# The router's products in four column groups with the gate stationary, and places counted by three products

## The reference, cut to what matters

```python
logits = xt @ gate_w.T                      # xt: 4096 x 256, gate_w: 8 x 256
scores = softmax(logits)
top_vals, idx = top_k(scores, 2)
weights = take_along_axis(scores, idx, axis=1)
xs = xt[:, None, :] * weights[:, :, None]
for e in range(8):
    mask = (idx == e)
    h  = silu(xs @ w1[e].T + b1[e])
    x2 = h @ w2[e].T + b2[e]
    x3 = xs @ w3[e].T + b3[e]
    y  = y + sum(x2 * x3 * mask)
z = silu(xt @ sw1.T) * (xt @ sw2.T) @ sw3.T  # the shared expert, for every token
out = x + gb * (y + z)
```

## Time and profile before

| | us |
|---|---|
| median of 3 runs | 2153.1 |
| span of the profiled execution, first to last instruction | 2151.5 |
| the stage of the change | about 1681 to 1900 |
| PE busy, whole span | 1868.9 (87%) |
| DVE busy, whole span | 1957.7 (91%) |
| ACT busy, whole span | 1522.9 (71%) |
| POOL busy, whole span | 1807.2 (84%) |

### The profile page before, as it was taken

How to read it: one execution, slowest core, us unless ns; L and a number is a source line. 1 busy time by engine, 2 the same in 40 slices (tenths; PEclk the granted TensorE clock), 3 DMA queues, 4 the chain that set the end, 5 groups by cost and what they waited for, 6 DMA issues and landing times.

```text
span 2151.5 us, 26056 instructions
## 1 busy us (share of the span) xinstructions
PE 1868.9 (87%) x6376; PEld 792.9 (37%) x6377; DVE 1957.7 (91%) x1814; ACT 1522.9 (71%) x3148; POOL 1807.2 (84%) x624
## 2 busy tenths in 40 slices
PE   7879898988889898989898888889775799999998
PEld 3323232323233332323232323333221466655554
DVE  7999999999999999999999999999999777557776
ACT  5786879798888879786878888887956333434443
POOL 5689999999999999999999999999999333415444
PEclk9998898989899898989898998989876899999999
DMA  6736445353625354454536263545334652234444
GB/s 261 248 108 159 104 125 124 101 127 102 153 73 149 96 142 109 124 123 110 129 101 140 80 156 88 135 109 129 98 102 134 237 186 79 107 82 79 78 78 70
DMA packets 140347, 265.32 MB, mean 123 GB/s; under 512 B 21264, under 2 KB 44048, under 8 KB 139072
## 3 DMA queue, kind: packets, MB, share of 16 engines
q1 hardware_dynamic: 125488, 242.05, 41.2%
q0 software_dynamic: 13440, 17.93, 4.9%
q10 hardware_dynamic: 1296, 3.93, 0.5%
HBM read 194.51 MB, written 70.39 MB: 123 GB/s over the span
## 4 chain that ended last, share of the span: by engine, by line
POOL 30%; PE 25%; issue 17%; ACT 14%; DVE 11%; DVEq 2%; DMA 0%; POOLq 0%; ACTq 0%; SPq 0%
POOL hst L940 21%; POOL dbu L928 7%; ACT psum L1257 6%; PE psum L2188 5%; PE psum L2031 4%; DVE hst L1611 4%; PE psum L2200 3%; PE psum L2251 2%; POOL dt L920 2%; PE psum L1951 2%; PE psum L1979 2%; DVE dbu L1590 1%; PE psum L1963 1%; ACT dbu L1289 1%; PE psum L2271 1%
## 5 line engine op out<-in xcount | busy, mean ns | idle before, releaser
L940 POOL TENSOR_TENSOR hst<-hst,c_rep 128x2048 f32<-128x2048 f32 x254 | 1143.7, 4521 | 4.2 <-ACT state L1243 4.2
L1611 DVE TENSOR_TENSOR_SCAN hst<-psum,state,dbu 128x1024 f32<-128x1024 f32 x384 | 878.8, 2330 | 6.2 <-ACT psum L1257 5.6
L1257 ACT ACTIVATE psum<-dt_rep,neg_a 128x512 f32<-128x512 f32 (+1 forms) x1024 | 659.8, 676 | 136.4 <-DVE hst L1611 131.4
L1590 DVE TENSOR_TENSOR dbu<-psum,b_rep 128x2048 f32<-128x2048 f32 x176 | 398.7, 2265 | 9.8 <-PE psum L2016 9.7
L928 POOL TENSOR_TENSOR dbu<-dtu_rep,b_rep 128x2048 f32<-128x2048 f32 x80 | 362.6, 4532 | 9.1 <-DMA dtu_rep<-dtu_scratch 4.9
L2031 PE MATMUL psum<-hst,same 128*32 128x512 f32 x2048 | 282.7, 701 | 84.1 <-POOL hst L940 77.9
L1611 DVE TENSOR_TENSOR_SCAN hst<-psum,dbu 128x1024 f32<-128x1024 f32 x128 | 286.4, 2272 | 11.9 <-ACT psum L1257 11.4
L2016 PE MATMUL psum<-dt,same 32*128 32x512 f32 x352 | 216.1, 696 | 91.4 <-DVE dbu L1590 85.8
L1963 PE MATMUL psum<-xp,taps 128*128 128x512 f32 x512 | 235.8, 604 | 7.3 <-ACT sp_tmp L1226 7.3
L1050 POOL DMA_INDIRECT out_x<-h,target_u x72 | 112.3, 1560 | 152.7 <-DMA out_x<-h,target_u 75.5
L2031 PEld LDWEIGHTS psum<-hst,same 128*32 128x32 f32 x2048 | 67.7, 126 | 306.6 <-issue 169.5
(11 more groups left out here) (186 smaller groups left out, 2512.8 us busy)
## 6 DMA issues: line engine op xcount, KB each, us to landing
dt_rep<-dt_scratch SPq DMA_DIRECT2D x256, 256.0 KB, 4.7
dtu_rep<-dtu_scratch SPq DMA_DIRECT2D x320, 64.0 KB, 1.9
taps<-taps_scratch SPq DMA_DIRECT2D x64, 256.0 KB, 4.4
b_rep<-bc_scratch SPq DMA_DIRECT2D x64, 256.0 KB, 5.0
c_rep<-bc_scratch SPq DMA_DIRECT2D x64, 256.0 KB, 7.7
dt_scratch<-dt SPq DMA_DIRECT2D x63, 256.0 KB, 5.4
h<-slot_scratch SPq DMA_DIRECT2D x72, 129.5 KB
sp_tmp<-t_scratch SPq DMA_DIRECT2D x16, 512.0 KB, 6.8
```

The lines of the kernel that those rows point to most:

```text
L940: nc.gpsimd.tensor_tensor(h, h, c_rep[q % 2][:], ALU.mult).then_inc(prod_done, 1)
L1257: nc.scalar.activation(psum[:, PS_A + i, kept], dt_rep[:, G % 2, j, kept], ACT.Exp, scale=neg_a[:, q % 2, u, i:i + 1]).then_inc(exp_done, 1)
L1590: nc.vector.tensor_tensor(dbu[:, U % DBU, :, :], psum[:, PS_U:PS_U + 1, :].broadcast_to((P, NG, TB)), b_rep[U // UNITS % 2][:], ALU.mult). ...
L1611: nc.vector.tensor_tensor_scan(both(hst[:, U % RING, groups, :]), both(psum[:, PS_A + 2 * pair:PS_A + 2 * pair + 2, :]), both(dbu[:, U % D ...
```

## The change

The gate is padded with zeros from 8 to 32 columns (GW = 32) and becomes the stationary operand. Each product moves 128 tokens of h2T through it and writes 32 partitions of bank 2: token tile tt goes to partitions 32 tt to 32 tt + 31, so the four tiles use the four column groups of the array. There are still 8 products. The logits now have experts on partitions. ScalarE copies the 128 x 128 out of PSUM (copy_logits), TensorE transposes it (turn_logits), and VectorE reads the logits from the result with a stride of 32.

On TensorE turn_logits(p) stands behind the gate half of the first shared chunk that follows router(p); turn_logits(0) stands right behind router(0). On ScalarE copy_logits(n) stands between silu_shared(0, n-1) and exp_scores(n).

The mask becomes three small tiles with zeroed leading rows: mask, pairs (each tile's mask plus the one before) and behind (pairs plus the pairs two back, so the sum of up to four tiles). rank_experts has two more chained instructions for it. count_places makes three products: `before` with row NT of `behind` broadcast over the four tiles, the identity with rows 0 to 3 of `behind`, and `ones` with row NT for the total. A block's pairs of one expert are thereby numbered partition by partition over all four tiles, where they were numbered tile by tile.

```diff
--- before.py
+++ after.py
@@ -34,6 +34,7 @@
 NE = 8
...
 ROWS = 2 * DS
+GW = P // NT
@@ -56,7 +57,7 @@
 LAST = NBLK - 1
...
 LATE = 4
-ROUTE = 8
+ROUTE = 10
@@ -284,7 +285,7 @@
         region = sb3("region", [P, NE])
...
         batch_flag = sb3("batch_flag", [P, BATCH, BATCH])
-        gate = sb3("gate", [P, KD, NE])
+        gate = sb3("gate", [P, KD, GW])
@@ -314,7 +315,10 @@
         rank = sb3("rank", [P, T3, NE])
...
         cmp_eq = sb3("cmp_eq", [P, NT, NE, NE])
-        mask = sb3("mask", [P, 2, NT + 1, NE])
+        turned_logits = sb3("turned_logits", [P, P])
+        mask = sb3("mask", [P, NT + 2, NE])
+        pairs = sb3("pairs", [P, NT + 2, NE])
+        behind = sb3("behind", [P, NT + 1, NE])
         place = sb3("place", [P, NT, NE])
@@ -444,6 +448,8 @@
         t_full = [sem("t_full0"), sem("t_full1")]
...
         f_logits = sem("f_logits")
+        l_full = sem("l_full")
+        l_copied = sem("l_copied")
         f_max = sem("f_max")
@@ -1452,6 +1458,10 @@
                 act.wait_ge(f_shift, p + 1)
...
+            def copy_logits(p):
+                act.wait_ge(l_full, p + 1)
+                nc.scalar.activation(turned_logits[:], psum[:, 2, P:2 * P], ACT.Copy).then_inc(l_copied, 1)
             def silu_shared(c, j):
@@ -1482,6 +1492,7 @@
                 if n > 0:
...
                     silu_shared(0, n - 1)
+                copy_logits(n)
                 exp_scores(n)
@@ -1651,7 +1662,7 @@
...
                 dve.wait_ge(f_logits, p + 1)
-                logits = psum[:, 2, 0:NT * NE].rearrange("p (t e) -> p t e", t=NT)
+                logits = psum[:, 2, 2 * P:3 * P].rearrange("p (t e) -> p t e", t=NT)[:, :, 0:NE]
                 nc.vector.tensor_reduce(fmax[:], logits, axis=AX_X, op=ALU.max).then_inc(f_max, 1)
@@ -1684,7 +1695,11 @@
                 chain(nc.vector.tensor_tensor(cmp_gt[:], cmp_gt[:], cmp_eq[:], ALU.add))
...
-                nc.vector.tensor_scalar(mask[:, p % 2, 0:NT, :], rank[:, rows_of(n), :], 1.5, None, ALU.is_lt
+                if p == 0:
+                    dve.wait_ge(mask_clear, 3)
+                chain(nc.vector.tensor_scalar(mask[:, 2:NT + 2, :], rank[:, rows_of(n), :], 1.5, None, ALU.is_lt))
+                chain(nc.vector.tensor_tensor(pairs[:, 2:NT + 2, :], mask[:, 2:NT + 2, :], mask[:, 1:NT + 1, :], ALU.add))
+                nc.vector.tensor_tensor(behind[:, 1:NT + 1, :], pairs[:, 2:NT + 2, :], pairs[:, 0:NT, :], ALU.add
                                         ).then_inc(a_mask, 1)
@@ -1702,10 +1717,10 @@
                 dve.wait_ge(a_placed, p + 1)
...
                 counted(nc.vector.tensor_tensor(
-                    place[:], psum[:, 2, NT * NE:2 * NT * NE].rearrange("p (t e) -> p t e", t=NT),
+                    place[:], psum[:, 2, 0:NT * NE].rearrange("p (t e) -> p t e", t=NT),
                     carry[:].rearrange("p (a e) -> p a e", a=1).broadcast_to((P, NT, NE)), ALU.add))
                 settle()
-                nc.vector.tensor_tensor(carry[:], carry[:], psum[:, 2, 2 * NT * NE:2 * NT * NE + NE], ALU.add
+                nc.vector.tensor_tensor(carry[:], carry[:], psum[:, 2, NT * NE:NT * NE + NE], ALU.add
                                         ).then_inc(a_taken, 1)
@@ -1782,8 +1797,8 @@
                 nc.vector.tensor_tensor(h, h, c_rep[(STEPS - 1) % 2][:], ALU.mult).then_inc(prod_done, 1)
...
             norm_statistics(0)
-            for half in range(2):
-                nc.vector.memset(mask[:, half, NT, :], 0.0).then_inc(mask_clear, 1)
+            for edge in (mask[:, 0:2, :], pairs[:, 0:2, :], behind[:, 0:1, :]):
+                nc.vector.memset(edge, 0.0).then_inc(mask_clear, 1)
             gate_y(STEPS - 1, NC - 1)
@@ -2155,39 +2170,44 @@
                     ins.then_inc(t_full[kd], 1)
...
             def router(n):
                 for kd in range(KD):
...
                     pe.wait_ge(a_taken, n)
-                for tt in range(NT):
-                    for kd in range(KD):
-                        ins = nc.tensor.matmul(psum[:, 2, tt * NE:(tt + 1) * NE],
-                                               h2T[:, n % 2, kd, tt * P:(tt + 1) * P], gate[:, kd, :],
-                                               start=(kd == 0), stop=(kd == KD - 1))
-                ins.then_inc(f_logits, 1)
+                for k in range(KD):
+                    for tt in range(NT):
+                        ins = nc.tensor.matmul(psum[GW * tt:GW * (tt + 1), 2, P:2 * P], gate[:, k, :],
+                                               h2T[:, n % 2, k, tt * P:(tt + 1) * P], start=(k == 0), stop=(k == KD - 1))
+                ins.then_inc(l_full, 1)
+            def turn_logits(n):
+                pe.wait_ge(l_copied, n + 1)
+                nc.tensor.transpose(psum[:, 2, 2 * P:3 * P], turned_logits[:], ident[:]).then_inc(f_logits, 1)
...
                 pe.wait_ge(a_mask, p + 1)
-                at = lambda tt: psum[:, 2, (NT + tt) * NE:(2 * NT + 1) * NE]
-                nc.tensor.matmul(at(0), before[:], mask[:, p % 2, :, :].rearrange("p t e -> p (t e)"),
-                                 start=True, stop=False)
-                for away in range(1, NT + 1):
-                    ins = nc.tensor.matmul(at(away), ones[:],
-                                           mask[:, p % 2, 0:NT + 1 - away, :].rearrange("p t e -> p (t e)"),
-                                           start=False, stop=(away == NT))
-                ins.then_inc(a_placed, 1)
+                places = psum[:, 2, 0:NT * NE].rearrange("p (t e) -> p t e", t=NT)
+                nc.tensor.matmul(places, before[:], behind[:, NT:NT + 1, :].broadcast_to((P, NT, NE)), start=True, stop=False)
+                nc.tensor.matmul(places, ident[:], behind[:, 0:NT, :], start=False, stop=True)
+                nc.tensor.matmul(psum[:, 2, NT * NE:NT * NE + NE], ones[:], behind[:, NT, :], start=True, stop=True
+                                 ).then_inc(a_placed, 1)
+            def shared_part(c, j, is_u):
+                bank, w, free, full = ((S_U[c % 2], sw2, s_u, s_u_full) if is_u else (S_G[c % 2], sw1, s_silu, s_g_full))
+                if NC * j + c > 1:
+                    pe.wait_ge(free, NC * j + c - 1)
+                if bank == S_O[1] and j > 0:
+                    pe.wait_ge(s_o_mul, 2 * j)
+                for k in range(KD):
+                    ins = nc.tensor.matmul(psum[:, bank, :], w[:, k, c * P:(c + 1) * P], h2T[:, j % 2, k, :],
+                                           start=(k == 0), stop=(k == KD - 1))
+                ins.then_inc(full, 1)
             def shared_hidden(c, j):
-                for bank, w, free, full in ((S_G[c % 2], sw1, s_silu, s_g_full), (S_U[c % 2], sw2, s_u, s_u_full)):
-                    if NC * j + c > 1:
-                        pe.wait_ge(free, NC * j + c - 1)
-                    if bank == S_O[1] and j > 0:
-                        pe.wait_ge(s_o_mul, 2 * j)
-                    for k in range(KD):
-                        ins = nc.tensor.matmul(psum[:, bank, :], w[:, k, c * P:(c + 1) * P], h2T[:, j % 2, k, :],
-                                               start=(k == 0), stop=(k == KD - 1))
-                    ins.then_inc(full, 1)
+                shared_part(c, j, False)
+                shared_part(c, j, True)
@@ -2208,19 +2228,23 @@
             turn(0)
...
             router(0)
+            turn_logits(0)
             pe.wait_ge(f_sw_loaded, 16 * 3)
...
             shared_hidden(1, 0)
-            pe.wait_ge(mask_clear, 2)
             count_places(0)
...
                 router(p)
-                for c in range(2 if p == 1 else 1, NC):
+                first = 2 if p == 1 else 1
+                shared_part(first, p - 1, False)
+                turn_logits(p)
+                shared_part(first, p - 1, True)
+                for c in range(first + 1, NC):
                     shared_hidden(c, p - 1)
@@ -2323,7 +2347,7 @@
         "b_conv": stack([on_partitions(w) for w in both("b_conv")]),
...
         "d_skip": stack([on_partitions(w) for w in both("D")]),
-        "gate": on_partitions(a["ffn_gate_w"].T),
+        "gate": on_partitions(np.pad(a["ffn_gate_w"].T, ((0, 0), (0, GW - NE)))),
         "sw1": on_partitions(a["ffn_sw1"].T),
```

## The result

The changed kernel takes 2168.57 us (median of 4 runs, 2167.68 to 2169.52) against 2153.19 us for the kernel before (4 runs, 2152.58 to 2153.84), a ratio of 1.0071 with a 95% interval of 1.0057 to 1.0085. It is slower by 15.4 us, where 6.9 were forecast and 2167 was the upper end of the range. The profiled execution has a span of 2166.0 us.

The account below looks back on a forecast made before the run. TensorE was taken to bound the stage by some 0.9 us over VectorE, except in block 1. 3.88 + 0.8 + 2.65 - 0.47 = 6.9 us on the 2151.5 span, plus 1.6 to the runs' median, gave 2160.0; range 2152 to 2167.

Parts of the forecast that it names:

- The sign, the place and the mechanism: Slower by 6.9 us, mostly in blocks 1 to 6: late logits and added mask instructions make VectorE delay shared_out.
- the clock's term: Block 1: TensorE idles some 5 us before its count, so half speed over one 1.8 us stretch costs 0.8 us.
- the loop: Last loop, over sorted tokens: the new order of an expert's pairs costs nothing, with 1 us either way.
- Blocks 2 to 6: Five blocks: later fmax and 0.44 us more mask work start shared_out at 17.94 for 17.41, 0.53 each, 2.65 in all.
- The router: TensorE's router products: four rounds at 0.13 us plus 0.18 for entering, 0.70 for 1.69; leaving costs 0.21.
- Block 1: Transposition behind a gate half waiting for silu at clock 0.53: fmax at 1716.10, shared_out 3.88 us later, block 0's gain included.
- Block 7: Last block, without VectorE statistics: the mask is ready near TensorE's count, shared_out follows u_sh at 16.94, 0.47 us less.
- Block 0: fmax at 1699.25 for 1699.40, mask and additions end at 1706.32, and the shorter count ends 0.37 us early.
- Rival 1: TensorE stays the bound: each block 1.1 us shorter, eight make 8.8 us, 2144.3; chance 0.12.
- Rival 2: Column groups overlap little with 128 columns: router 1.71 + 0.18 us, sum 14.0 us slower, 2167.1; chance 0.10.
- Rival 3: Mode changes and loads hidden, block 1 at full clock, fmax by 6.6: 1.4 us slower, 2154.5; chance 0.18.

Follow-up runs that it names:

- The filler: Changed kernel plus five 128x128 products, results unused, on TensorE ahead of count_places in blocks 2 to 7: 2163.25 us, ratio 1.0039.
- VectorE's order mended: Changed kernel with norm_statistics ahead of shift_logits, rank_experts ahead of shared(1, p-1), block 1's transposition ahead of its gate half: 2147.57 us, ratio 0.9975.
- block 1's logits first: Changed kernel with the transposition of block 1 alone ahead of the gate half that waits for the silu: 2165.24 us, ratio 1.0051.
- router only: Changed kernel with the old mask and count (one mask, five products): 2159.47 us, ratio 1.0021.
- statistics first: Changed kernel with VectorE's norm_statistics(p+1) ahead of shift_logits(p), nothing else moved: 2155.43 us, ratio 1.0008.
- transposition at once: Changed kernel with turn_logits(p) right behind router(p) in every block: 2151.83 us, ratio 0.9990.

## Why the prediction was wrong

- The sign, the place and the mechanism were right, the size wasn't. The failed step is the clock's term, "the half speed of one such stretch of 1.8 us costs 0.8", set once and for block 1 alone. I had TensorE idle ahead of the count in blocks 2 to 6 and did not ask what that does to the clock. There it cost 3 x 1.69 = 5.07 us in the first trace and 4 x 1.69 = 6.8 in the second. In block 1, where I had added the 0.8, shared_out lost nothing in the first trace and 1.69 in the second. The filler, which takes away the pause and nothing else, kept every shared_out that it stands before at 7.2.
- Against the 6.9 us that were forecast, the 14.5 of the spans are 7.6 more: 5.07 - 0.8 for the clock, 0.8 in blocks 2 to 6 and 0.2 in block 7 for shared_out behind a pause (below), 0.4 before the stage, 0.1 in blocks 0 and 1, and 1.8 in the loop, which I had put at nothing with 1 us either way. Without the clock's 5.07 us the 2168.57 would be 2163.5, inside the range.
- Blocks 2 to 6 were forecast 0.53 us longer and are 0.67 to 0.73 without the clock. shared_out did start at 17.94 behind the turn. What I missed is that it takes 7.17 and not 7.01 us when it starts behind a pause.
- The router was forecast at 0.70 us and takes 0.58: four rounds at the pace of the matmuls (0.11 each) and some 0.13 for entering; leaving costs 0.19 (1.91 for 1.72). fmax came at 6.94 for 7.08. Loads are hidden beside matmuls on the same rows in the short rounds too (the trace has the router's 16 loads within 0.38 us, beside its products). By the rule of the Trainium skill that I weighed (TensorE: Matmul & The Clock Gate, Packing small matmuls), that loads overlap with matmuls in flight only when the row group differs, the four rounds would take 4 x 0.24 = 0.96 us, an estimate, and the trace disagrees with its 0.58.
- Block 1: fmax at 1716.47 for a forecast of 1716.10, of which 0.35 is the later start of the stage (ScalarE's copy of project_out at 1698.06 for 1697.71); the first shared_out 20.24 behind the turn for 15.71. The gate half found the lower clock, as forecast. Shown by moving one call: 3.26 us.
- Block 7: forecast -0.47, measured -0.31; the 0.16 is shared_out behind a pause again (7.17 for 7.01). Block 0: -0.37, measured -0.45 when the stage's later start is taken off (turn(1) at 1707.32 for 1707.42 in the chain).
- The new order of places costs nothing that the runs show: the loop takes 252.1 to 255.1 us in the 12 traces, 252.1 to 254.0 with the old order and 252.1 to 255.1 with the new. The 1.8 us between the changed kernel and the kernel before are within that spread, and why the loop's length varies stays open.
- Rival 1 (TensorE stays the bound) needed fmax not to be late. With VectorE's order mended it came true for 0.9 of its 1.1 us a block. Rival 2 (groups that overlap little) gave 2167.1, nearest to the measured time, by luck: its router of 1.9 us was 0.58. Rival 3 needed fmax by 6.6 us, and it came at 6.94.

## What to carry to other kernels

When work is taken off the engine that seems to be the bound, follow the result to its consumer: here the products got 1.1 us shorter and their result 0.9 us later, since it now went through two more engines and stood behind cover on the queue. Take the consumer's slack from its idle time (0.9 us), and sum on its side before summing on the other. An edit that is free alone can cost much beside another: the new count cost 0.3 us with the old router and 8.7 with the new one, whose late logits had used up VectorE's slack. Once a pause appears on TensorE, price it twice, for itself and for the clock after it; and look for idle time ahead of the late result, into which work behind it can be moved.

## What the runs showed of the hardware

TensorE's granted clock was 0.52 in the 3.45 us behind two pauses of 1.25 and 0.37 us, in blocks in which it was else busy throughout. In blocks 2 to 6 this happened to 3 of 5 shared_outs in the changed kernel's first trace, to 4 of 5 in its second, and to 3 of 5 with block 1's logits first. It happened to none behind a pause of 0.80 us (router only), behind 0.24 and 0.37 (statistics first), behind 0.40 and 0.27 (transposition at once), or with the 1.25 us filled. So five products whose result nobody reads made the kernel 5 us faster (2163.25 us for 2168.57).

The router's 16 records of 128 columns in four column groups take 0.57 us. A round of four takes 0.11 us, no more than a single record of that width in the filler's sequence (ten in 1.28 us, the last of which is recorded with 0.27: 1.01 / 9). That leaves 0.13 for entering the four groups (worked out, not seen by itself).

shared_out's 32 records take 7.01 us when TensorE was at work up to them and 7.17 behind a pause.
